# Which key tiles VectorE adds for GpSimd, and a stream of row maxima that runs one tile ahead, in an attention and FFN block on one core

## The reference

```python
xn = layernorm(x)
x + attn(xn, Wq, Wk, Wv, Wo) + ffn(xn, w_gate, w_up, w_down)

# attn: 16 heads of 64; K and V are projected to 512 columns and every
# column repeated twice; rope on q and k; full softmax, no mask
scores = softmax(rope(xn @ Wq) @ rope(xn @ Wk).T * 2.0)
out = (scores @ v) @ Wo
# ffn: h = silu(xn @ wg.T) * (xn @ wu.T);  out = h @ wd.T   (int8-like weights times 1/127)
```

## Time and profile before

| what | value |
| --- | --- |
| three runs | 1169.87 us median (1164.29 to 1173.73) |
| the profiled execution | 1166.32 us, span 1164.4 us |
| granted TensorE clock, mean | 0.989 of full speed |
| TensorE busy | 1118.8 us, 96% of the span |
| VectorE busy | 886.7 us, 76% |
| GpSimd busy | 877.2 us, 75% |
| ScalarE busy | 733.7 us, 63% |

### The profile page before, as it was taken

One profiled execution on the slowest core, in us unless ns is written; L12 is line 12 of the kernel. 1 busy time (PEld: TensorE's weight loads), 2 busy tenths in 40 slices (PEclk: granted clock), 3 DMA queues, 4 the chain that ended last, 5 costly groups with the idle time before them and its releaser, 6 DMA issues.

```text
span 1164.4 us, 17083 instructions
## 1 busy us (share of the span) xinstructions
PE 1118.8 (96%) x6288; PEld 661.8 (57%) x6288; DVE 886.7 (76%) x1009; ACT 733.7 (63%) x1330; POOL 877.2 (75%) x274
## 2 busy tenths in 40 slices
PE   5899999999999999999999999999999999999986
PEld 4787555555555565555555555555556555554432
DVE  7686777778787887778787887778788787777721
ACT  3333666666676666766666666666666666666663
POOL 3222778887778888877778887878778887888776
PEclk9899999999999999999999999999999999999999
DMA  6662808071441618071441618071431617050000
GB/s 230 167 258 87 238 2 224 1 222 40 111 115 35 191 37 224 2 222 40 115 110 39 187 37 224 1 218 44 122 105 45 181 37 225 1 130 2 4 1 18
DMA packets 56305, 124.97 MB, mean 107 GB/s; under 512 B 7968, under 2 KB 19488, under 8 KB 54048
## 3 DMA queue, kind: packets, MB, share of 16 engines
q1 hardware_dynamic: 56224, 123.89, 36.8%
HBM read 53.08 MB, written 10.49 MB: 55 GB/s over the span
## 4 chain that ended last, share of the span: by engine, by line
PE 80%; DVE 15%; ACT 2%; issue 1%; POOL 1%; DMA 1%; POOLq 0%; ACTq 0%; DVEq 0%
PE bank_o L394 20%; PE bank_s L542 19%; PE scores L379 18%; DVE row_max L853 13%; PE scores L361 7%; PE bank_m L369 3%; PE bank_m L430 2%; PE bank_m L407 2%; PE bank_m L404 2%; ACT prob L799 2%; PE scores L480 2%; PE bank_s L497 1%; POOL prob_sum L1048 1%; PE bank_o L497 1%; PE bank_m L497 1%
## 5 line engine op out<-in xcount | busy, mean ns | idle before, releaser
L799 ACT ACTIVATE prob<-bank_s 128x512 f32<-128x512 f32 x1024 | 595.5, 600 | 253.4 <-PE bank_s L542 230.0
L853 DVE TENSOR_REDUCE row_max<-scores 128x1 f32<-128x1024 f32 x512 | 597.0, 1214 | 201.3 <-PE scores L379 201.1
L1048 POOL TENSOR_TENSOR prob_sum<-prob_sum,prob 128x2048 f32<-128x2048 f32 x96 | 439.3, 4576 | 13.9 <-ACT prob L799 0.5
L542 PE MATMUL bank_s<-qk_pack 98*128 98x512 f32 x1024 | 431.0, 437 | 8.2 <-ACT prob L799 5.9
L379 PE MATMUL scores<-qk_pack 96*128 96x512 f32 x1024 | 337.4, 411 | 9.0 <-DVE row_max L853 1.4
L542 PEld LDWEIGHTS bank_s<-qk_pack 98*128 98x128 f32 x1024 | 192.9, 189 | 195.1 <-issue 86.9
L394 PE MATMUL bank_o<-prob,v 128*32 128x512 f32 x2048 | 250.0, 606 | 0.0
L1048 POOL TENSOR_TENSOR prob_sum<-prob_sum,prob_pair 128x2048 f32<-128x2048 f32 x32 | 147.2, 4601 | 104.3 <-DVE prob_pair L946 104.3
L379 PEld LDWEIGHTS scores<-qk_pack 96*128 96x128 f32 x1024 | 180.1, 190 | 73.8 <-DVE row_max L853 52.3
L992 POOL TENSOR_TENSOR qk_stage<-rope,qk_stage 128x512 fp32r<-128x512 f32 x64 | 82.0, 1283 | 91.1 <-ACT qk_stage L685 91.1
L1040 POOL TENSOR_TENSOR prob_sum<-prob 128x2048 f32<-128x2048 f32 x32 | 146.8, 4587 | 0.0
(11 more groups left out here) (88 smaller groups left out, 685.0 us busy)
## 6 DMA issues: line engine op xcount, KB each, us to landing
qk_pack<-qk_stage SPq DMA_DIRECT2D x384, 128.0 KB, 4.7
table<-tables SPq DMA_DIRECT2D x16, 2048.0 KB, 9.7
w_stage<-w_scratch SPq DMA_DIRECT2D x14, 640.0 KB, 4.5
v<-v_stage SPq DMA_DIRECT2D x32, 256.0 KB, 7.9
xT_scratch<-xT_hl SPq DMA_DIRECT2D x4, 1024.0 KB, 10.1
x_stage<-xT_scratch SPq DMA_DIRECT2D x4, 1024.0 KB, 6.5
w_scratch<-w_split SPq DMA_DIRECT2D x1, 2560.0 KB, 15.5
x_all<-x SPq DMA_DIRECT2D x4, 512.0 KB, 11.7
```

Source lines behind the costliest of these rows:

```text
L542: mm(bank_s[:, h % 2, :], qk_pack[j][0:SCORE_K, 1, kt // QT, h, (kt % QT) * 128:(kt % QT + 1) * 128], qk_pack[j][0:SCORE_K, 0, t, h, :], s ...
L799: A(prob[:, kt % RING, h, :], bank_s[:, h % 2, :], ACT.Exp).then_inc(prob_ready, 1)
L853: V.tensor_reduce(row_max[:, m:m + 1], scores[:, at:at + 2, :].rearrange("p c k -> p (c k)"), axis=AX.X, op=ALU.max).then_inc(max_read, 1)
L1048: TT(prob_sum[:, t], prob_sum[:, t], part, ALU.add).then_inc(sum_done, 1)
```

## The change

It has these parts.
1. `pair_sum` adds key tiles 0 and 1 instead of 4 and 5, directly into prob_sum, and VectorE issues it after the reduction of tile 7 of its unit instead of after the normalisation. prob_pair is gone.
2. GpSimd's `add_probs` starts from that sum and adds key tiles 2, 3, 4, 5, 6: five additions, as before, each waiting for its key tile.
3. The stream of maxima is one tile ahead: after score(7, 3) of unit u TensorE computes tile 0 of the maxima of unit u + 2, and unit u + 1 goes on with tile 1. One call of `maxima` goes from kt = 4, and the one at kt = 5 comes before score(5, 1), the transposes of the inverses after it. The wait for the packed operands moves with it, from the unit's start to after score(7, 3).
4. `invert` comes after tile 10 instead of 9.
5. ScalarE's two `round_hi` come after the exponentials (1, 0) and (1, 1) instead of (1, 1) and (2, 1), and the ring's waits follow the new readers.

```diff
-INVERT_AFTER = 9
+INVERT_AFTER = 10
+PAIR_AFTER = 7
 # TensorE
+            tiles = [iter(range(TILES)) for _ in range(UNITS)]
-                def maxima():
-                    if do_max:
-                        m = next(tiles)
+                def maxima(v=v, v_n=v_n, v_t=v_t):
+                    if v < UNITS:
+                        m = next(tiles[v])
                         if m < 2:
-                            pe.wait_ge(rope_done, capped(2 * u + 7 + m, 2 * UNITS))
+                            pe.wait_ge(rope_done, capped(2 * v + 5 + m, 2 * UNITS))
                         max_tile(v, m, v_n, v_t)
-                if do_max and t == 1:
-                    pe.wait_ge(packed, 16 * PACKS * (s + 1))
                 for kt in range(KT):
...
                         score(kt, 2)
                         maxima()
                         score(kt, 3)
-                        maxima()
                     elif kt == 5:
+                        maxima()
+                        score(kt, 1)
                         if not is_first(u):
                             transpose_inv(u - 1)
-                        score(kt, 1)
-                        maxima()
                         score(kt, 2)
                         maxima()
                         score(kt, 3)
+                        if is_first(u):
+                            maxima()
...
                         score(kt, 3)
+                        if t == 0 and v + 1 < UNITS:
+                            pe.wait_ge(packed, 16 * PACKS * (s + 1))
+                        maxima(v + 1, 1 - j, t)
 # ScalarE
-                        if kt < 2:
-                            act.wait_ge(pair_done, u)
-                        elif kt == 2:
-                            act.wait_ge(sum_done, 5 * u)
+                        if kt < 3:
+                            act.wait_ge(sum_done, 5 * u + kt - 2)
                         elif kt == 3:
                             act.wait_ge(den_ready, u)
                         elif kt < 6:
-                            act.wait_ge(sum_done, 5 * u + 1)
+                            act.wait_ge(pair_done, u + 1)
                         else:
-                            act.wait_ge(sum_done, 5 * u + kt - 4)
+                            act.wait_ge(sum_done, 5 * u + kt - 5)
...
+                        elif (kt, h) == (1, 0) and staged:
+                            round_hi(0, u + 3, 1 - t, s + 1 + t)
                         elif (kt, h) == (1, 1) and staged:
-                            round_hi(0, u + 3, 1 - t, s + 1 + t)
+                            round_hi(1, u + 3, 1 - t, s + 1 + t)
                         elif (kt, h) == (1, 3) and not is_second(u):
                             read_y(u - 2)
-                        elif (kt, h) == (2, 1):
-                            if staged:
-                                round_hi(1, u + 3, 1 - t, s + 1 + t)
-                            if not first:
-                                read_den(u - 1)
+                        elif (kt, h) == (2, 1) and not first:
+                            read_den(u - 1)
 # VectorE
-            def pair_sum(u):
-                dve.wait_ge(prob_ready, NE * (KT * u + 6))
-                at_least(dve, sum_done, 5 * u - 1)
-                V.tensor_tensor(prob_pair[:], prob[:, 4 % RING], prob[:, 5 % RING], ALU.add).then_inc(pair_done, 1)
+            def pair_sum(u, t):
+                dve.wait_ge(prob_ready, NE * (KT * u + 2))
+                at_least(dve, den_ready, u - 1)
+                V.tensor_tensor(prob_sum[:, t], prob[:, 0], prob[:, 1], ALU.add).then_inc(pair_done, 1)
...
                         reduce_tile(u + 1, m)
+                        if m == PAIR_AFTER:
+                            pair_sum(u, t)
                         if m == INVERT_AFTER and not is_first(u):
                             invert(u - 1)
                     split_max(u + 1)
                 else:
+                    pair_sum(u, t)
                     invert(u - 1)
                 if not is_first(u):
                     normalise(u - 1)
-                pair_sum(u)
 # GpSimd
             def add_probs(u, t):
-                at_least(pool, den_ready, u - 1)
-                pool.wait_ge(prob_ready, NE * (KT * u + 2))
-                TT(prob_sum[:, t], prob[:, 0], prob[:, 1], ALU.add).then_inc(sum_done, 1)
-                for n, kt in enumerate((2, 3, 4, 6)):
-                    if kt == 4:
-                        pool.wait_ge(pair_done, u + 1)
-                    else:
-                        pool.wait_ge(prob_ready, NE * (KT * u + kt + 1))
-                    pool.wait_ge(sum_done, 5 * u + n + 1)
-                    part = prob_pair[:] if kt == 4 else prob[:, kt % RING]
-                    TT(prob_sum[:, t], prob_sum[:, t], part, ALU.add).then_inc(sum_done, 1)
+                pool.wait_ge(pair_done, u + 1)
+                for n, kt in enumerate(range(2, KT - 1)):
+                    pool.wait_ge(prob_ready, NE * (KT * u + kt + 1))
+                    at_least(pool, sum_done, 5 * u + n)
+                    TT(prob_sum[:, t], prob_sum[:, t], prob[:, kt % RING], ALU.add).then_inc(sum_done, 1)
```

More of the change, by code:

```diff
@@ L134, in build @@
         prob_sum = keep("prob_sum", [128, 2, HG, HALF])
[L135 to L138, removed]
+        wgu = keep("wgu", [128, 2, 2 * HT, 128], F32R)
+        wdn = keep("wdn", [128, HT, D])
         xn = [v_sb[min(c // 2, 1)][:, c % 2 * QT:(c % 2 + 1) * QT, :] for c in range(CHUNKS)]
@@ L536, in slot @@
                 do_max = not (last_pair and j == 1 and t == 1)
-                tiles = iter(range(TILES))
                 def score(kt, h):
@@ L620, in slot @@
                         score(kt, 3)
+                    elif kt == 5:
                         maxima()
-                    elif kt == 5:
+                        score(kt, 1)
                         if not is_first(u):
                             transpose_inv(u - 1)
-                        score(kt, 1)
-                        maxima()
                         score(kt, 2)
@@ L987, in _, with split_lo @@
             TT = nc.gpsimd.tensor_tensor
-            def split_lo(w, t):
-                for k in range(2):
+            def split_lo(w, t, chunks=range(2)):
+                for k in chunks:
                     pool.wait_ge(hi_done, 2 * w + k + 1)
@@ L1059, in slot @@
                 u = 4 * i + 2 * j + t
-                if not (last_pair and (j, t) != (0, 0)):
+                staged = not (last_pair and (j, t) != (0, 0))
+                if staged:
                     split_lo(u + 3, 1 - t)
```

## The result

| | before | changed |
| --- | --- | --- |
| median | 1171.62 us (4 runs) | 1307.07 us (4 runs, 1307.01 to 1307.37) |
| ratio | | 1.118, 95% interval 1.113 to 1.122 |
| profiled execution, span | 1164.4 us | 1305.1 us |
| mean granted TensorE clock | 0.989 | 0.946 |

Slower by 12%. The page of the changed kernel: busy time and granted clock, then the chain that ended last, by engine, then two groups of instructions (busy and mean ns, then the engine's idle time before them and who ended it).

What follows compares the result with a forecast made beforehand. TensorE's hand-written order was taken to bound the kernel. 1166.3 + 21.6 (unit changes) + 69.8 (stalled transposes) + 2 (last unit) gave 1259.7, say 1260 us; own range 1235 to 1290, with 8 in 10 for 1150 to 1310.

Steps and rivals of the forecast that it cites:

- Part 2, the collision: VectorE's cast of split_max waits for GpSimd's third addition (shared SBUF ports); TensorE's transpose of maxima stalls 2.25 us per unit.
- Rival A: The subtraction after the cast loses the gap between two GpSimd additions and waits a whole one more: 1406 us; chance 12%.
- Rival B: The cast is not held up, or its wait is hidden, say by other phases: 1190 us; chance 14%.
- Part 1: VectorE's pair sum of 2.28 us fits into its idle hole during the denominators and costs nothing.
- Part 3: Stream one tile ahead: start of a unit + 0.81 us with three tiles in a row, key tiles 4 and 5 - 0.34.
- Part 5: Both roundings before exponential (1, 2) make score (2, 0) later: + 0.25 us, bounds 0 and + 0.6.
- The sum: Unit start, roundings and key tiles 4 and 5: 0.81 + 0.25 - 0.34 = 0.72 us for 30 changes of unit, 21.6 us.
- the price of the stall: TensorE's stall at the transpose of the maxima counted as 2.25 us for each of 31 transposes: 69.8 us.
- + 2: In the last unit GpSimd's five additions can start only after key tile 2: + 2 us.
- Rival C: Faster: TensorE's waits for reductions and rotate vanish, the cast meets a gap of GpSimd: 1130 us (1115 to 1165); chance 12%.

Runs made afterwards that it cites:

- experiment 1: The changed kernel with GpSimd's addition of key tile 4 waiting until VectorE's cast and subtraction are done: 1198.34 us, ratio 1.023 to the kernel before.
- experiment 2: The changed kernel with GpSimd's first addition waiting for two more exponentials, so its five additions run later: 1199.19 us, ratio 1.023 to the kernel before.
- experiment 3: The changed kernel with TensorE's transpose of the maxima moved behind the third projection: 1229.25 us, ratio 1.050 to the kernel before.
- experiment 7: The kernel before with only the pair sum moved, and GpSimd's addition of key tile 4 waiting for the cast and subtraction: 1175.14 us, ratio 1.003.
- experiment 5: The kernel before with only ScalarE's two roundings moved to (1, 0) and (1, 1): 1175.49 us, ratio 1.004.
- the kernel that yields: The changed kernel with GpSimd waiting for VectorE's cast and subtraction before adding key tile 4, the same run as experiment 1: 1198.34 us.
- experiment 6: The kernel before with only the pair sum moved (tiles 0 and 1, after the reduction of tile 6), GpSimd adding 2 to 6: 1244.3 us, ratio 1.063.

## Why the prediction was right, and where it was off

The direction and the cause were right, and so was the unit's time where the clock stayed up. The total was 47 us low: 1307 lies outside the 1235 to 1290 given for this mechanism, and is within the 1150 to 1310 by 3 us only. That was luck, for nothing in that range stood for what added the time.

**Part 2, the collision.** Forecast: the cast at 3.74 us, the transpose 16.94 us after score (2, 2), a stall of 2.25 us. Measured in the unit shown (score (2, 2) at 568.64): 3.80, 585.53 - 568.64 = 16.89, and 2.20. TensorE was idle before 30 transposes, not 31: the first two casts took only 0.17 and 0.64 us. Before the last three it was idle for 2.7 us. Experiments 1, 2 and 3 show each link: which addition is running, that the cast waits for it, that TensorE's transpose carries the wait on. Rival A is out: the subtraction took 0.17 us in all 32 cases. Rival B's case, another phase of GpSimd's chain, is what experiment 2 made, and it gave 1199 for B's 1190.

**Part 1.** The pair sum fits: 2.28 us, and VectorE was still idle for 0.62 us before reduction 8.

**Part 3.** The start of a unit takes 596.60 - 591.58 = 5.02 us against 4.13, + 0.89 for a forecast of + 0.81; key tiles 4 and 5 take 4.20 us, - 0.35 for - 0.34. One reason in it was wrong: I counted 0.3 us of the present start as waits, part of it for rope. By experiment 7 nothing of that goes when rope is early.

**Part 5.** + 0.27 by experiment 5, forecast + 0.25. **The sum** of these three was 0.72; the kernel that yields has units of 33.47 us, + 0.81.

**The step that failed is the price of the stall.** I wrote that a stall of 2.25 us costs 2.25 us, and left TensorE's clock out of the sum. A unit with full clock took 35.7 us, as forecast (35.6). But in 23 of 31 the clock fell after the idle stretch, 1.57 us each: 36 us. Most of the rest is at both ends: the last three distances between transposes grew by 14.3 us, not by 8.9 (one of the 23 is among them), the first by 4.7, not by 3.0. After the last transpose it is 55.8 us against 51.3, for which + 2 stood. The trace of the kernel before had a warning, for its own clock fell at the start of the attention, 112 us into the span, after TensorE had been idle for 0.90 us for a DMA and 0.88 us for an exponential; I did not put it into the sum.

**Rival C** is out. With VectorE free of the pair at the unit's end and no collision, a unit is 32.67 us (experiment 7). VectorE's idle time had no price in this kernel, and the tile ahead makes a row of three tiles, of which the third waits.

## What to carry to other kernels

When GpSimd runs long operations back to back, ask of each VectorE instruction that was seen to wait for them, even the smallest, where in GpSimd's chain it will be issued: a 0.17 us cast waited 3.8 us, and 1.4 us of delay on the other engine undid it. A "busy" VectorE instruction whose mean is far above its minimum is such a wait. And price a stall of TensorE with what the clock does after it: here one of 2.2 us cost 3.8 in most units.

## What the runs showed of the hardware that I had not expected

- The clock is not simply a matter of whether TensorE waits. Idle stretches of 2.03 us before the transpose brought it down in most units, 1.73 us (experiment 6) in every fourth or fifth, 0.48 us in none of the full units. The length of the stall does not decide between equal units of one kernel: in the four full units of the changed kernel that followed a stall and had no low stretch, TensorE had been idle for 2.03 to 2.08 us, as in the others. What does decide was not tried.
- The wait between VectorE and GpSimd goes both ways: GpSimd's 1.28 us addition took 3.34 us when it came behind a pair sum that was waiting already.
- In the last units, which have no projections, the clock can fall where TensorE does not wait at the transpose: the last two distances are at 0.90 and 0.90 in experiment 7, 1.00 and 0.90 in experiment 1, 1.00 and 1.00 in experiment 2 and in the kernel before. Each is one profiled execution, and the cause is open.
